# Edge stage of a graph layer: one wait of GpSimd for every four quads of gathers in place of one for each quad

## The reference, cut to what matters

```python
feat_all = jnp.einsum('ni,rhid->rnhd', inputs, conv_weights)      # node stage
feat_src_e = feat_all[edge_type, edge_src]                        # one row of 256 per edge: the gathers
...
e = jax.nn.leaky_relu(el + er, negative_slope=LEAKY_SLOPE)
m = jax.ops.segment_max(e, edge_dst, num_segments=N_NODES)
ex = jnp.exp(e - m[edge_dst])
denom = jax.ops.segment_sum(ex, edge_dst, num_segments=N_NODES)
alpha = ex / denom[edge_dst]
h = jax.ops.segment_sum(alpha[..., None] * feat_src_e, edge_dst, num_segments=N_NODES)
```

## Time and profile before

| | |
|---|---|
| time, median of 3 runs | 2474.11 us (2470.37 to 2475.55) |
| span of the profiled execution, first to last instruction | 2456.4 us |
| median less the span | 17.7 us |
| edge stage, about | 244 to 1882 us of the span |
| gathers of the edge stage | 996 |

### The profile page before, as it was taken

The page is one execution under the profiler, slowest core; times in us unless marked ns, Lnnn a source line. Parts: engine busy times, 40 slices in busy tenths (PEclk is TensorE's granted clock), DMA queues, the critical chain, the costliest instruction groups (busy, mean ns, idle before and its releaser), DMA issues. The chain is left out here.

```text
span 2456.4 us, 35279 instructions
## 1 busy us (share of the span) xinstructions
PE 1898.8 (77%) x9138; PEld 1594.8 (65%) x9139; DVE 1062.3 (43%) x3018; ACT 1076.9 (44%) x3259; POOL 1142.0 (46%) x1164
## 2 busy tenths in 40 slices
PE   8999125767767777867777777677877689999998
PEld 7887124656655665656565666565665668999887
DVE  6332013545555555545555555455567532221111
ACT  2222123645555545554555555454656532222221
POOL 4000744556666566666666566656620443122222
PEclk9999556787877768777787777777788689999999
DMA  6443422333333333333333333333312877777774
GB/s 239 189 170 143 109 67 74 84 90 88 90 92 92 88 88 91 90 88 90 88 92 92 89 90 90 92 85 88 91 44 80 282 230 221 248 246 247 241 234 104
DMA packets 121157, 315.51 MB, mean 128 GB/s; under 512 B 27047, under 2 KB 71335, under 8 KB 106180
## 3 DMA queue, kind: packets, MB, share of 16 engines
q0 software_dynamic: 60192, 149.24, 23.4%
q1 hardware_dynamic: 60836, 164.88, 19.3%
HBM read 257.36 MB, written 57.71 MB: 128 GB/s over the span
## 5 line engine op out<-in xcount | busy, mean ns | idle before, releaser
L798 POOL DMA_INDIRECT gath<-feats,idxT x996 | 950.6, 954 | 799.1 <-issue 272.7
L1154 PE MATMUL psP<-gath,hot 128*128 128x260 f32 x1992 | 668.1, 493 | 28.6 <-DVE gath L905 15.1
L1154 PEld LDWEIGHTS psP<-gath,hot 128*128 128x128 f32 x1992 | 469.4, 247 | 123.5 <-issue 35.4
L1113 PE MATMUL psOT<-cst,hot 128*128 128x128 f32 x996 | 196.1, 331 | 346.0 <-ACT hotT L1045 231.9
L1045 ACT COPY hotT<-psOT 128x512 f32<-128x512 f32 x249 | 143.5, 576 | 628.6 <-remote 485.4
L1113 PEld LDWEIGHTS psOT<-cst,hot 128*128 128x128 f32 x996 | 139.7, 171 | 407.2 <-issue 309.0
L1138 PEld LDWEIGHTS psE<-er,hotT 128*128 128x128 f32 x1992 | 309.7, 235 | 48.6 <-issue 44.9
L914 DVE TENSOR_TENSOR acc<-acc,psP 128x260 f32 x498 | 211.0, 424 | 295.3 <-remote 127.9
L1138 PE MATMUL psE<-er,hotT 128*128 x1992 | 309.5, 305 | 31.1 <-issue 19.9
L1035 ACT ACTIVATE hot<-cst,ndlT 128x128 f32<-128x128 f32 x996 | 316.2, 391 | 4.7 <-PEq L325 4.7
L1680 ACT ACTIVATE acc<-psH,w1buf 128x256 f32<-128x256 f32 (+1 forms) x344 | 122.4, 423 | 346.7 <-PE psH L1571 304.3
(11 more groups left out here) (232 smaller groups left out, 1178.5 us busy)
## 6 DMA issues: line engine op xcount, KB each, us to landing
w1buf<-in_experts SPq DMA_DIRECT2D x43, 1030.0 KB
w2buf<-in_experts SPq DMA_DIRECT2D x43, 1024.0 KB
feats<-frow SPq DMA_DIRECT2D x29, 1040.0 KB, 3.9
gath<-feats,idxT POOLq DMA_INDIRECT x996
meta<-in_edges SPq DMA_DIRECT2D x464, 12.0 KB
acc<-slots_x SPq DMA_DIRECT2D x23, 258.0 KB
gath<-in_b SPq DMA_DIRECT2D x43, 128.0 KB
acc<-slots_x SPq DMA_DIRECT2D x20, 129.0 KB
```

What stands on the lines that cost most here:

```text
L798: pool.indirect_dma_start(gath[:, r, u], None, feats, bass.IndirectOffsetOnAxis(ap=idxT[:, r, u:u + 1], axis=0)).then_inc(gath_in[r], 16)
L1113: ins = pe.transpose(psOT[:, k * P:(k + 1) * P], hot[:, r, j * QUAD + k], ident)
L1154: ins = pe.matmul(psP[:, bank(g, b, r), 0:FW], hot[:, r, u], gath[:, r, u], start=u % BLK == 0, stop=u % BLK == BLK - 1)
```

## The change

GpSimd's wait for freed buffers is made once for four quads, and then for the last of the four. For group g it waits, ahead of quad 0, until quad 3 of group g - 3 is summed, and ahead of quad 4, until quad 7 is. In the last group (five quads) the second wait is for its only remaining quad. The gathers, their order and their number stay as they are.

```diff
         PQ = QUAD // BLK
+        TOGETHER = 4
...
                     for j in range(quads(g)):
-                        if not isinstance(g, int) or g >= GBUFS:
-
-                            wait_apart(pool, sum_ready, freed(g, j), carrier)
+                        if j % TOGETHER == 0 and (not isinstance(g, int) or g >= GBUFS):
+
+                            wait_apart(pool, sum_ready, freed(g, min(j + TOGETHER, quads(g)) - 1), carrier)
                         for u in range(j * QUAD, (j + 1) * QUAD):
                             pool.indirect_dma_start(gath[:, r, u], None, feats,
                                                     bass.IndirectOffsetOnAxis(ap=idxT[:, r, u:u + 1], axis=0)).then_inc(gath_in[r], 16)
```

## The result

The changed kernel takes 2856.5 us (median of 4 runs, 2856.07 to 2862.46) against 2472.2 us for the kernel before (4 runs, 2468.71 to 2475.55): a ratio of 1.1559, with a 95% interval of 1.1532 to 1.1586. I had predicted 2474 us with 76% on no change and the worst of my rivals at 2503. The loss of 384 us is far outside all of them.

The account below looks back on a forecast made before the run. It took a loop of TensorE, ScalarE and VectorE in the edge stage to bound the kernel, with GpSimd ahead. Terms 0 + 0 + 0 kept the span at 2456.4 us, plus 17.7 around it: 2474 us (76%), range 2466 to 2483.

Parts of the forecast that it names:

- the worst of my rivals: Edge stage: gathers land too late for their reader, a microsecond short in each of 29 groups, 29 us, 2503 us; chance 2%.
- What bounds the kernel: Edge stage: TensorE, ScalarE and VectorE wait for each other, none for the gathers; one period is 49.8 us.
- the loop that I described: Edge stage: TensorE's transposes wait for ScalarE's copies, these for the transposes, VectorE's chain for TensorE's small products.
- Removed, worth 0 on the path: GpSimd's queue from group 3: 171 waits and increments go, costing only its idle time, with 9.5 us a period to spare.
- The sign of being wrong that the prediction named: Wrong if L838 waits for a DMA, or the period changes over 0.15 us with VectorE's three small steps unchanged.
- Moved: Gathers of quads 0 to 2 and 4 to 6 start later, ending at most 15.1 us later; cost 0 on the path.
- Beside other work: Edge stage: traffic in a run of 16 gathers stays as inside a quad, mean 87 GB/s; cost taken as 0.
- That rival: VectorE's serial chain: gather runs hold its three small steps (L847, L862, L863), up to 14.3 us, 2488 us; chance 5%.
- 83 us on these steps: VectorE's 87 small steps: by the port rule each could be held for a gather's full 0.95 us.
- The rhythm: Edge stage: TensorE's clock levels shift, 7 us either way, 2467 or 2481 us; chance 14%, half to each side.
- The 17.7 us around the span: Whole kernel: time added to the profiled span of 2456.4 us to reach the median of 2474.1 us.
- The range: Whole kernel: 2466 to 2483 us, past both turns of the clock and into VectorE's held chain, leaving out some 12%.

## Why the prediction was wrong, step by step

- *What bounds the kernel:* I took "nobody waits for the gathers" for "nobody waits for GpSimd". The first is right, before and after (0.2 us of idle time before the reader in both). The second isn't: the other engines wait for GpSimd to stop. I also read only those waits that named an instruction. ScalarE's "remote", 370.0 us in 59 waits, was left out, the largest in the same window and larger than any row shown from it, and so were the 50.3 us of its longest wait and VectorE's 67.3 us, both at the opening. All three stand in the kernel before, and none is explained by the loop that I described.
- *Removed, worth 0 on the path:* this is the step that failed. The waits, at some 2.5 us of idle time each where they were true waits (204.7 us by 83 and 121.8 by 46), were priced as idle time of an engine that is ahead. They were the gaps in which TensorE's updates got through. The price is 14.4 us a period from group 4 to 28, and 390 us from the first L838 to the last. The sign of being wrong that the prediction named came true in its second form: the period changed by far more than 0.15 us, and the steps of the earlier trace rows didn't slow down.
- *Moved:* right, as far as it says that the gathers still come in time. For group 16 the last gather ends at 1272.8 and the reader starts at 1341.7, 69 us of margin, more than the 42 forecast, because the period grew.
- *Beside other work:* I said that traffic in a run is what it is now inside a quad. It is, and it doesn't matter: half the rows changed nothing for the better, and plain DMAs of the same bytes hold no update. What I didn't ask is what else a run of gathers may touch; I had read only VectorE's small steps. That rival falls. The steps take less time in the mean than before, not more:

```profile
L864 DVE TENSOR_SCALAR lv<-lv 4x32 f32<-4x32 f32 x29 | 5.6, 194 | 1.0
L863 DVE TENSOR_SCALAR lv<-lv 4x32 f32<-4x32 f32 x29 | 5.2, 178 | 0.0
L848 DVE COPY cat<-seg 128x2 f32<-128x2 f32 x29 | 4.9, 169 | 1.0
```

- The Trainium skill's rule on the port that VectorE and GpSimd share ("SBUF — State Buffer", "Who interferes with whom") would at most have given, by the prediction's estimate, 83 us on these steps, and by another mechanism. The trace doesn't agree with a loss of that size: these three steps got shorter in the mean, and their longest is 394 ns (411 before).
- *The rhythm:* the granted clock of the stage fell from 0.77 to 0.70. TensorE's busy time rose only from 1056.6 to 1067.6 us for nearly the same matmuls, so the clock is a small part. It fell together with TensorE's busy share of the stage, 75% to 59%; no run varies it by itself.
- *The 17.7 us around the span:* this isn't what lies around it. Of the changed kernel, time and span of one execution are on record: 2856.39 and 2854.6 us, 1.8 us apart. So the profiled execution of the kernel before was a short one, about 2458 us by estimate, and most of the 17.7 us is the difference between executions. The forecast of 2474 was the measured median and isn't touched. But the short execution is why the two spans differ by 398 us and the medians by 384.
- *The range:* all its ends were prices of things that the trace had named. Nothing in it stood for the one resource that the change alters most, the pattern of GpSimd's idle time.

What stays open: which unit holds TensorE's updates, and why gathers do it and plain DMAs don't (they differ in the looked-up rows and in GpSimd's time for each, 0.95 against 0.54 us; these weren't varied one by one). All runs say when it happens, none says where. The ends of matmuls in the trace are modelled, so it can't be told either whether the update alone is late or the end of the work that makes it. Whether GpSimd doing other work between gathers would let the updates out, as its idle time does, wasn't tried.

## What to carry to other kernels

Idle time of an engine that is off the path can still be doing something for the others; before a change closes such gaps, look at what the other engines do at the moments when they open. When two engines that wait for different instructions of a third start within 0.1 us of each other, suspect a common hold that is released there, and find what ended just before. And a wait whose releaser the profile can't name is the first to be explained, above all when it is the largest of its engine.

## What the hardware showed that I had not expected

- While GpSimd issues indirect DMAs back to back (1.26 us each), TensorE's semaphore updates are held, for up to some 18 us in runs of 16 and 37 in runs of 32, and come in a bundle after the run: 1.3 to 1.8 us after the last of 8 gathers, 2.7 to 3.1 after 16, 4.8 to 5.1 after 32. The last packet of the gathers is over 1.5 us after the last of them in all three. VectorE's and ScalarE's updates go on (1 of 766 over 0.5 us late in the changed kernel, against 167 of TensorE's 387). Single updates of TensorE do get through in a long run (one at 1359.66 in the stretch above).
- Plain DMAs of GpSimd, 0.54 us each, do nothing of the kind in runs of 16 or of 32 (0 of 809 late in both), with the same bytes and as many packets.
- Half the rows in a gather take GpSimd 0.91 us in place of 0.95: its time for a gather hardly goes by the rows.
- A wait that is already met doesn't let the updates out (ratio 1.158); idle time of some 2.5 us after each 8 gathers, spent in a wait for their landing, does (1.015).
